# Waits ahead of the indirect additions onto the output: which of them the DMA itself carries, how often the others are made, and where the index limit is loaded

## What is computed

```python
x = x + gnn(xn, edge_index, ...) + mix(xn, ...)       # attention over edges, linear attention and MLP
x = x + ffn(layernorm(x), ...)                        # ffn, per node:
probs = softmax(xf @ gate_w + gate_b)                 # 8 experts
top2_vals, top2_idx = top_k(probs, 2)                 # two experts a node
h = gelu(xf @ w1 + bb1); y = h @ w2 + bb2             # for each expert
out = out + we[:, None] * y                           # weighed by the gate
```

## Time and profile before

| | |
|---|---|
| median of three runs | 3321.4 us (3318.71 to 3327.85) |
| the profiled execution | 3321.79 us, its span 3320.5 us |
| mean granted TensorE clock | 0.908 of full speed |
| POOL busy | 2242.3 us, 68% of the span |
| the L2270 DMAs | 210, 333.8 us busy, 299.1 us idle before them |

### The profile page before, as it was taken

How to read it: one execution, slowest core, us unless ns; L and a number is a source line. 1 busy time by engine, 2 the same in 40 slices (tenths; PEclk the granted TensorE clock), 3 DMA queues, 4 the chain that set the end, 5 groups by cost and what they waited for, 6 DMA issues and landing times.

```text
span 3320.5 us, 42453 instructions
## 1 busy us (share of the span) xinstructions
PE 2669.9 (80%) x11566; PEld 2081.3 (63%) x11566; DVE 2013.9 (61%) x5421; ACT 1554.9 (47%) x3383; POOL 2242.3 (68%) x2200
## 2 busy tenths in 40 slices
PE   8657767898889888888888875664289998889997
PEld 6546545565666656566665654443268787778886
DVE  7445566676777767777776766776446455444221
ACT  5335544555555554555555544332245554444442
POOL 0277777777777777777777777773657776666444
PEclk9879988999999999999999988777599999999998
DMA  9797766666666666666656666655757676666553
GB/s 274 244 295 205 199 172 165 172 162 177 170 179 171 174 164 172 184 168 182 170 162 177 169 168 169 162 152 158 252 122 163 160 166 153 130 132 140 98 90 45
DMA packets 399210, 562.00 MB, mean 169 GB/s; under 512 B 72713, under 2 KB 319519, under 8 KB 398794
## 3 DMA queue, kind: packets, MB, share of 16 engines
q0 software_dynamic: 124704, 298.62, 35.6%
q1 hardware_dynamic: 197033, 171.49, 17.9%
q10 hardware_dynamic: 77161, 88.52, 10.1%
HBM read 403.25 MB, written 170.61 MB: 173 GB/s over the span
## 4 chain that ended last, share of the span: by engine, by line
PE 56%; DMA 13%; POOL 9%; ACT 8%; issue 7%; DVE 6%; ACTq 1%; SPq 0%; POOLq 0%; DVEq 0%
PE bank L1284 21%; DMA rows<-table,srcix 9%; PE bank L1083 7%; PE bank L2185 6%; PE bank L2198 6%; PE bank L1072 5%; POOL rows L1220 5%; DMA out<-x_y,x_dest 2%; POOL sorted_d L1724 2%; PE bank L1045 2%; PE bank L593 1%; PE bank L594 1%; PE bank L853 1%; POOL out L2270 1%; ACT L1324 1%
## 5 line engine op out<-in xcount | busy, mean ns | idle before, releaser
L1220 POOL DMA_INDIRECT rows<-table,srcix x1661 | 1598.0, 962 | 506.1 <-issue 357.7
L1284 PE MATMUL bank<-rows,onehot 128*128 128x272 f32 x3328 | 923.6, 425 | 57.7 <-ACT fout L1338 52.4
L1338 ACT ACTIVATE fout<-bank 128x272 f32<-128x272 f32 x1664 | 640.8, 397 | 569.7 <-PE bank L1284 521.4
L1284 PEld LDWEIGHTS bank<-rows,onehot 128*128 128x128 f32 x3328 | 665.6, 207 | 243.5 <-ACT fout L1338 78.3
L1430 DVE TENSOR_TENSOR rows<-rows,bank 128x1024 f32<-128x1024 f32 x416 | 484.0, 1213 | 169.3 <-ACT rows L1329 169.0
L2270 POOL DMA_INDIRECT out<-x_y,x_dest x210 | 333.8, 1589 | 299.1 <-DMA out<-x_y,x_dest 149.2
L2185 PE MATMUL bank<-x_int,x_w1c 128*128 128x256 f32 x1680 | 395.5, 390 | 20.2 <-issue 12.6
L2198 PE MATMUL bank<-e_w,x_ht 128*128 x1680 | 388.4, 385 | 6.8 <-DVE x_y L2251 4.0
L2185 PEld LDWEIGHTS bank<-x_int,x_w1c 128*128 128x128 f32 x1680 | 327.9, 196 | 70.8 <-issue 24.0
L2223 ACT ACTIVATE x_ht<-bank,x_b1c 128x256 f32<-128x256 f32 x420 | 174.3, 471 | 378.2 <-PE bank L2185 378.0
L2198 PEld LDWEIGHTS bank<-e_w,x_ht 128*128 128x128 f32 x1680 | 316.3, 193 | 50.9 <-issue 10.7
(11 more groups left out here) (376 smaller groups left out, 3256.7 us busy)
## 6 DMA issues: line engine op xcount, KB each, us to landing
frag<-fout ACTq DMA_DIRECT2D x104, 544.0 KB
x_in<-sorted_d SPq DMA_DIRECT2D x105, 260.0 KB, 3.4
rows<-table,srcix POOLq DMA_INDIRECT x1661
x_b2c<-in_L_ffn_b SPq DMA_DIRECT2D x105, 128.0 KB, 3.7
frag<-in_x ACTq DMA_DIRECT2D x1, 13416.0 KB
table<-hr SPq DMA_DIRECT2D x24, 544.0 KB, 4.2
xs<-in_x SPq DMA_DIRECT2D x24, 512.0 KB, 6.1
xg<-in_x SPq DMA_DIRECT2D x24, 512.0 KB, 6.6
```

The costliest lines, as they stand in the source:

```text
L1220: p.indirect_dma_start(out=B.rows[b][:, j, :], out_offset=None, in_=B.table[:, :], in_offset=bass.IndirectOffsetOnAxis(ap=B.srcix[:, col:c ...
L1284: pe.matmul(B.banks[2 + c % 3][:, 0:ROW], B.onehot[k % 2][:, j, :], B.rows[k % NR][:, j, :], start=True, stop=True).then_inc(S.sum, 1)
L1338: a.activation(B.fout[k % 2][:, j, :], B.banks[2 + c % 3][:, 0:ROW], ACT.Copy).then_inc(S.ev, 1)
```

## The change

`store` now names the wait for the last landing first and DVE's second; the waits for the plain stores are made only in a round's first store; and the index limit is put into a register once, ahead of all stores.

```diff
 def experts_pool(p, S, B):
+    bound = p.alloc_register("last_node")
+    p.reg_mov(bound, N_NODES - 1)
+
     def store(j):
 
         r = ROUND_OF[j]
-        p.wait_ge(S.x_st, 2 * j + 2)
-        for q in range(max(r - NF + 1, 0), r + 1):
-            p.wait_ge(S.e_x1[q % NF], stored_to(q))
         if j:
             p.wait_ge(S.x_y[(j - 1) % NOUT], 32 * ((j - 1) // NOUT + 1))
+        p.wait_ge(S.x_st, 2 * j + 2)
+        if j == 0 or r > ROUND_OF[j - 1]:
+            for q in range(max(r - NF + 1, 0), r + 1):
+                p.wait_ge(S.e_x1[q % NF], stored_to(q))
         for i in range(SUB):
             p.indirect_dma_start(out=B.out[:, :], out_offset=bass.IndirectOffsetOnAxis(ap=B.dest[j % (NOUT + 1)][:, i:i + 1], axis=0),
-                                 in_=B.y[j % NOUT][:, i, :], in_offset=None, bounds_check=N_NODES - 1, oob_is_err=False,
+                                 in_=B.y[j % NOUT][:, i, :], in_offset=None, bounds_check=bound, oob_is_err=False,
                                  compute_op=ALU.add).then_inc(S.x_y[j % NOUT], 16)
```

## The result

| | before | changed |
|---|---|---|
| median | 3321.34 us | 3300.86 us |
| runs | 3318.71 to 3327.85 | 3297.18 to 3304.95 |
| profiled execution: time, span, granted clock | 3321.79, 3320.5, 0.908 | 3302.54, 3301.3, 0.913 |

The account below looks back on a forecast made before the run. POOL's serial stores, each waiting for the previous landing, were taken to bound the end. Gains of 15.2 us there and 3 in the route's stretch, 18.2 together, gave 3303.2 us against the median; range 3294 to 3316.

Parts of the forecast that it names:

- The link: Time from a store's landing to the next store's first DMA on POOL: 0.28 instead of 0.86 us, 0.58 less per store.
- Rows 7 and 8: Profile rows where POOL's first L1724 and first L732 carry a wait themselves and start 0.28 us after it.
- The lower bound: If the DMA were worked on only after its wait, the link would be 0.72 us, 0.14 us less per store.
- That POOL has caught up with DVE about six tiles before the end: At the end, POOL's 14.9 us backlog is less than the 20.9 us that 36 shorter steps save.
- Rival (b): Transfers take back the link's gain: landings from 4.1 to 4.7 us leave only 3 us, 3318 us; chance 5%.
- The tail's term: Stores at the kernel's end: last store starts at about 3300.5 instead of 3315.75, gain 15.2 us, between 14.4 and 15.9.
- The route's stretch: From 2390 to 3054 us: gain of 3 us that shifts PE's whole stream, bounds 0 and 13.
- What costs nothing: At the stores: plain-store waits once a round cover later stores; without this 0.04 us each, hidden by the landing.
- (a): At the stores, the DMA is worked on only after its wait: 0.14 us gained a store, 3316 us; chance 11%.
- (c): Slower: moved steps in the route's stretch give PE other idle times and its clock falls, 3332 us; chance 4%.
- (d): Change doesn't do what it says: waits or register hold POOL elsewhere, link stays 0.86, 3321 us; chance 3%.

Follow-up runs that it names:

- order and register: Kernel before with landing waited for last and the limit in a register, plain stores still waited for at every store; 3299.3 us, ratio 0.9932.
- the resident kernel: Changed kernel with b2 of all eight experts loaded into SBUF once, DVE picking the tile's by a register; 3288.5 us, ratio 0.9902.

## Why the prediction was right, and where it was off

**The link: right.** The taken value was 0.28 instead of 0.86; it is 0.266 instead of 0.856. Rows 7 and 8, two DMAs of other kinds, bore it. The lower bound, a link of 0.72, is near what each half of the change leaves alone (0.77 and 0.78). Additions with a limit in a register behave as L1724 does, 0.266 us from the event to the start against its 0.28.

**That POOL has caught up with DVE about six tiles before the end: wrong.** The last store still waited for its landing, 5.1 us behind DVE and not 3. The store's backlog was 31.0 us at tile 70, as before (31.3), and fell to 5.1 at the last. The step that failed is the assumption that transfers keep their length. They went from 4.06 to 4.26 us, so that of 0.59 us less in the link a mean of 0.20 was taken back (steps 6.82 to 6.46, not to 6.3). Nor did POOL's steps come to follow PE's 7.35 us a tile (3285.77 less 3278.42 in the earlier trace rows; from 3053 to 3297 us PE was busy for 243.29 of 244.00 us, at a granted clock of 1.00). With the changed kernel's own DVE times and its link, but the transfers of before, the stores worked through one by one would have caught up at tile 97 to 100, as forecast. In "order and register", with the same link and transfers of 4.17, POOL did catch up, at the last but one tile, and its lag is 2.1. Rival (b) had this mechanism with three times the size; its sign, a median landing of 4.7 in the window of the earlier trace rows, is 4.2 after 4.1. The tail's term was 15.2 and is 12.9 us (18.0 less 5.1).

**The route's stretch: right in kind, too small.** 3 us were taken between bounds of 0 and 13; PE ends at 3290.0 instead of 3296.3, so 6.3. I had counted only the landings that stood on the chain. DVE's waits for landings at L2239 in this stretch (2390 to 3050 us), of before and of the changed kernel, are 8.7 us shorter:

```profile
DVE x_dest L2239 <- DMA out<-x_y,x_dest: 76.8, 18, 8.0
```

```profile
DVE x_dest L2239 <- DMA out<-x_y,x_dest: 68.1, 15, 7.9
```

From 2390 to 3300 us they fell by 62 us, from 205.6 to the 143.5 above, but most of that lies behind 3050 us, where PE didn't wait for it. The 6.3 us are read from one run of each kernel and are uncertain: in the three kernels with a part of the change and a link of 0.77 to 0.83, PE ends at 3290.5 to 3298.8. That the link gave something here is likely: counted from PE's first matmul on x_in, PE ends 900.1 and 896.1 us later in the two kernels with a link of 0.266 (changed, order and register) and 902.3 to 907.2 us later in the kernel before and the three parts. How much isn't shown. The two errors, 2.3 too much in the tail and 3.3 too little here, nearly cancel: 12.9 + 6.3 = 19.2, the difference of the two spans, against 18.2 forecast. That they cancel is luck.

**What costs nothing: right.** Making the waits for plain stores once a round changed no time alone (3320.5 us), nor did their return (order and register: 3299.3 against 3300.9).

**The rivals.** (a) fell by the link; its 3316 us is what order or register alone gives (3317.5, 3316.2). (b) was true in part, above. (c): the granted clock is 0.913, not under 0.908. In the trace of before the slow batch of the earlier trace rows, from 2754.87 to 2760.25 us, ran at a granted clock of 0.68, and the stretch from 3278 to 3282 us, in which the first fast one of the earlier trace rows lies, at 1.00. (d) fell by the link.

**What stays open.** The long transfers go with fetches of x_in and b2 in flight, and leaving out the loads of b2 shortens the mean. Why a transfer that meets both takes 4.31 us before, 4.64 in the changed kernel and 5.12 with twelve buffers for x_dest, and why eight for x_y brought the mean back to 4.05, wasn't settled. What DVE's load of the register costs the resident kernel as a whole wasn't isolated either.

## What to carry to other kernels

Where one instruction's DMA is chained to the landing of the one before, look at the program as built. Here the link was 0.266 us where the semaphore that comes last was the one that the DMA itself carries, 0.77 where a MOVE that loads the limit stood between and took the wait, and 0.78 where the DMA carried another wait. Both parts were needed; half of it gave nothing that could be told from noise. And a serial chain that bounds the end hides a gain in front of it: 26 us of PE were worth nothing behind a link of 0.86, while the same buffers gave 14 us behind one of 0.27, so shorten the chain first, then add buffers. Leaving out the later b2 loads, which shortened the transfers in the chain itself, gave 17 us with either link.

## What was not expected of the hardware

- A wait that stands in an instruction of its own ahead of an indirect DMA costs 0.5 to 0.6 us more than one that the DMA carries: 0.77 to 0.86 against 0.266 us from landing to start. Of this, 0.49 to 0.53 is the sequencer's work on one DMA in most stores (0.81 in the last one shown above), and the link of 0.266 leaves no room for it behind the event: where the wait is the DMA's own, it is done ahead.
- The link is constant: 0.266 or 0.265 us in 31 of the last 34 stores of the changed kernel, while the transfers vary from 2.7 to 5.6 us.
- A store's second DMA took 3.4 us to land where no fetch of x_in or b2 was in flight beside it, in all four kernels sorted above, and 4.3 to 5.1 where both were.
- 100 loads of 128 KB, with SP's wait ahead of them, were worth 17 us in a kernel whose DMA engines' share is 0.53 to 0.64 in these stretches.
